# One ring slot's reload moved behind the team's last down product, in a mixture-of-experts stage on one Trainium2 core

## The reference

```python
router_logits = x @ gate_w                                   # 256 x 64
routing_weights, selected = jax.lax.top_k(router_logits, 8)
routing_weights = jax.nn.softmax(routing_weights, axis=-1)
...
gate = jax.lax.ragged_dot(hidden_sorted, gate_proj_w, group_sizes)    # 64 experts, 512 x 192
up = jax.lax.ragged_dot(hidden_sorted, up_proj_w, group_sizes)        # 64 experts, 512 x 192
down = jax.lax.ragged_dot(jax.nn.silu(gate) * up, down_proj_w, group_sizes)   # 192 x 512
...
out = jnp.sum(out * routing_weights[..., None], axis=1)
return x + out
```

## Time and profile before

| | |
|---|---|
| median of 3 runs | 325.79 us |
| the profiled execution, device time | 328.78 us |
| its span, first to last instruction | 327.1 us |
| TensorE busy in the span | 301.1 us, 92% |
| VectorE busy | 166.9 us, 51% |
| ScalarE busy | 100.7 us, 31% |
| mean granted TensorE clock | 0.974 of full |
| weights and other data moved by SP's queue | 83.51 MB |

### The profile page before, as it was taken

One profiled execution on the slowest core, in us unless ns is written; L12 is line 12 of the kernel. 1 busy time (PEld: TensorE's weight loads), 2 busy tenths in 40 slices (PEclk: granted clock), 3 DMA queues, 4 the chain that ended last, 5 costly groups with the idle time before them and its releaser, 6 DMA issues.

```text
span 327.1 us, 8833 instructions
## 1 busy us (share of the span) xinstructions
PE 301.1 (92%) x2667; PEld 170.6 (52%) x2667; DVE 166.9 (51%) x567; ACT 100.7 (31%) x198; POOL 77.2 (24%) x183
## 2 busy tenths in 40 slices
PE   0499999989899999799999999999999999999994
PEld 0364444435577545436555655565556555655561
DVE  7752366495468585424534453445344534453443
ACT  1020400212748134313333333333333323332332
POOL 5000000340000033442233224222422233223322
PEclk9999999999669999959999999999999999999999
DMA  2699995930000010691999999999999999999921
GB/s 70 242 429 397 386 394 193 373 108 2 2 0 4 0 42 25 217 376 43 358 386 390 392 382 392 353 394 393 385 393 390 373 371 387 385 394 384 392 85 66
DMA packets 42363, 87.85 MB, mean 269 GB/s; under 512 B 6023, under 2 KB 14351, under 8 KB 42208
## 3 DMA queue, kind: packets, MB, share of 16 engines
q1 hardware_dynamic: 39600, 83.51, 68.9%
q0 software_dynamic: 2320, 3.95, 3.4%
q10 hardware_dynamic: 416, 0.04, 0.1%
HBM read 90.09 MB, written 1.05 MB: 279 GB/s over the span
## 4 chain that ended last, share of the span: by engine, by line
PE 83%; DVE 9%; ACT 3%; issue 2%; POOL 1%; POOLq 1%; DVEq 0%; ACTq 0%
PE psum L1343 22%; PE psum L1399 17%; PE psum L1273 10%; PE psum L1091 5%; PE psum L1130 4%; PE psum L1103 4%; PE psum L1386 4%; PE psum L1380 2%; PE psum L1191 2%; PE psum L1221 2%; PE psum L1082 2%; ACT store L971 2%; PE psum L1175 1%; PE psum L1245 1%; PE psum L1366 1%
## 5 line engine op out<-in xcount | busy, mean ns | idle before, releaser
L1343 PE MATMUL psum<-store 128*32 128x384 f32 x896 | 80.1, 496 | 0.6 <-issue 0.6
L1399 PE MATMUL psum<-store 128*32 128x256 f32 (+1 forms) x672 | 54.9, 459 | 0.4 <-DVE store L888 0.4
L1343 PEld LDWEIGHTS psum<-store 128*32 128x32 f32 x896 | 35.1, 112 | 33.3 <-issue 30.2
L902 DVE SCALAR_TENSOR_TENSOR y_parts<-psum,w_slot,y_parts 128x512 fp32r<-128x512 f32 x28 | 21.0, 751 | 54.4 <-ACT y_parts L1045 54.4
L1045 ACT ACTIVATE y_parts<-psum,w_slot 128x512 fp32r<-128x512 f32 x28 | 19.2, 687 | 57.0 <-PE psum L1399 52.9
L1273 PE MATMUL psum<-y_parts,place_T 128*128 128x512 f32 x112 | 33.8, 422 | 0.9 <-ACT y_parts L1045 0.8
L1399 PEld LDWEIGHTS psum<-store 128*32 128x32 f32 x672 | 23.0, 110 | 20.1 <-issue 8.5
L571 POOL DMA_INDIRECT store<-x_normed_rows,row_no x29 | 29.7, 1024 | 15.0 <-issue 15.0
L1273 PEld LDWEIGHTS psum<-y_parts,place_T 128*128 128x128 f32 x112 | 18.8, 188 | 21.2 <-DVE y_parts L902 14.2
L570 POOL TENSOR_TENSOR ready<-zero 128x1 f32<-128x1 f32 x29 | 5.6, 193 | 98.2 <-DVE row_no L869 98.2
L1013 ACT ACTIVATE store<-psum 128x512 f32<-128x512 f32 x29 | 17.3, 597 | 34.8 <-PE psum L1386 31.7
(11 more groups left out here) (247 smaller groups left out, 398.8 us busy)
## 6 DMA issues: line engine op xcount, KB each, us to landing
store<-n_L_ffn_gate_proj_w_dram SPq DMA_DIRECT2D x64, 384.0 KB
store<-in_L_ffn_up_proj_w_dram SPq DMA_DIRECT2D x64, 384.0 KB
store<-n_L_ffn_down_proj_w_dram SPq DMA_DIRECT2D x64, 256.0 KB
store<-n_L_ffn_down_proj_w_dram SPq DMA_DIRECT2D x64, 128.0 KB
store<-in_L_attn_w_qkv_dram SPq DMA_DIRECT2D x1, 3072.0 KB, 15.0
store<-in_ctx_dram SPq DMA_DIRECT2D x2, 1024.0 KB, 6.5
store<-in_L_attn_w_out_dram SPq DMA_DIRECT2D x1, 1024.0 KB, 17.3
x_sb<-in_x_dram SPq DMA_DIRECT2D x1, 512.0 KB, 4.4
```

Source lines behind the costliest of these rows:

```text
L902: dve.scalar_tensor_tensor(y_parts[:, 1], bank[6], w_slot[:, :], y_parts[:, 0], ALU.mult, ALU.subtract).then_inc(s_yl, 1)
L1343: last = pe.matmul(bank[0][quarter, 0:2 * INTER], xs[:, c, quarter], w[:, :, c, :], start=(c == 0), stop=(c == DC - 1))
L1399: last = pe.matmul(bank[6][quarter, cols], hidT[:, k, quarter], ring[r][:, e, at:at + cols.stop - cols.start], start=(k == 0), stop=(k == 2))
```

## The change

`reload` waits once, for `s_y`, and then issues the 16 transfers of the slot lane by lane: gate, up and the two down parts of expert 0, then those of expert 1, and so on. Sizes, addresses and semaphores of the transfers stay as they were, and so do the loads of teams 0 to 3 and all other engines.

```diff
-            def load_gate_up(team, r):
+            def load_gate_up(team, r, first=0):
                 loaded = []
-                for j, e in enumerate(team):
+                for j, e in enumerate(team, first):
                     loaded.append(e)
                     lane = ring[r][:, j]
...
-            def load_down(team, r):
-                for j, e in enumerate(team):
+            def load_down(team, r, first=0):
+                for j, e in enumerate(team, first):
                     lane = ring[r][:, j]
...
                 team = list(team_of(word_of(q)))
-                sp.wait_ge(s_gu, sp.snap(done))
-                load_gate_up(team, r)
                 sp.wait_ge(s_y, sp.snap(done))
-                load_down(team, r)
+                for j, e in enumerate(team):
+                    load_gate_up([e], r, j)
+                    load_down([e], r, j)
```

## The result

The changed kernel took **331.89 us**, the median of 4 runs (328.76 to 333.33), beside 325.88 us before: ratio 1.0195, 95% interval 1.0137 to 1.0253. It is slower by 6.0 us, in the range and to the side that was given, 2.2 us over the point. The profiled execution took 333.33 us, span 331.6. The title names one ring slot; the edit is to all 12 calls of `reload`, and it changes the order of each one's 16 transfers as well as the wait.

A forecast was written before the change was run, and what follows sets the result against it. TensorE was taken to bound the last stage. The stream 3.97 us later and gate and up 3.3 us further back, against 3.5 us of slack, gave a 3.8 us stall: 325.8 + 3.9 = 329.7 us, range 325.4 to 333.6.

The forecast's parts named there:

- What bounds the kernel: Last stage: TensorE bounds it, a round every 6.547 us; the transfers only have to keep ahead.
- The wait moves the stream by 3.97 us and nothing absorbs it: First reload starts at 157.6, not 153.65; the transfers end 3.97 us later; later waits cause no second loss.
- one slowest DMA engine that never runs dry: Weight stream: the slowest of 16 engines sets the pace, from 155 to 315 us with nothing missing, 13.35 us a team.
- The order adds 3.3 us for gate and up: End of each reload: 1.1 us of transfers behind the last gate and up instead of 4.4, so they land 3.3 us later.
- the slack of 3.5 us: Last round: gate and up there at about 310.8, wanted at 314.33, leaving 3.5 us.
- The clock taken at 0: TensorE behind the last round's stall: half clock could cost 0 to 2.9 us; 0 was taken.
- rival B: Last round: stall plus half clock behind it, 329.7 + 2.9 = 332.6 us; chance 0.30.
- A: Last round: no stall outside the profile, time unchanged at 325.8 us; chance 0.27 together with the edit doing nothing.
- C: Reloads: mixed row sizes run a few per cent slower on the slowest engine, 334 to 337 us; chance 0.06.
- D: Expert rounds: less load on SBUF shortens each of 25 rounds by 0.04 us, 324.8 us or less; chance 0.04.

The follow-up runs named there:

- experiment 5: Kernel before with the wait for s_y ahead of gate and up in the first reload alone: 326.38 us, ratio 0.9988, runs in two heaps.
- experiment 7: Changed kernel with each of GpSimd's indirect fetches of token rows replaced by a memset: 327.37 us, one run.
- Experiment 2: Kernel before with one wait for s_y ahead of every reload, transfers in the old order: 327.15 us, ratio 1.0058.
- experiment 3: Kernel before with the new wait and lane-by-lane order in the last team's reload alone: 326.07 us, ratio 1.0029.
- experiment 9: Changed kernel with 5 useless matmuls in TensorE's 1.08 us self attention gap: 327.66 us.
- 11: Kernel before with the later wait alone, old order, plus 5 useless matmuls in the self attention gap: 323.04 us.
- experiment 8: Kernel before with 5 useless matmuls in TensorE's 1.08 us self attention gap: 321.63 us, ratio 0.9898.
- 12: Kernel before with 5 useless matmuls in the self attention gap and 5 in the 1.27 us gap of the first round of experts: 321.38 us, ratio 0.986.
- 6: Changed kernel with the last team's 16 transfers back in the old order behind the same wait: 326.83 us, ratio 1.0035.
- 1: Changed kernel run again without edit: 331.76 us, median of 6 runs.
- 4: Changed kernel with 18 useless matmuls ahead of the last team's wait for gate and up: 329.69 us.
- 10: Changed kernel with 5 useless matmuls in the self attention gap and 18 in the gap ahead of the last round: 325.99 us.

## Why the prediction came out as it did

**What bounds the kernel**: right. TensorE kept its beat of 6.55 us in every round but the last.

**The wait moves the stream by 3.97 us and nothing absorbs it**: right. The data end 4.1 us later against the beat, the first reload is issued 154.81 - 150.65 = 4.16 us behind the third round's gate and up, as forecast (157.6 - 153.45), and experiment 5 shows that the first reload alone brings a gap of the same kind. The cause I gave for it, one slowest DMA engine that never runs dry, is shown in part: experiment 5's tail has one engine of 16 at work alone. That this engine was busy without a pause since round 3 was only argued, as the profile has no view by engine, and experiment 7 leaves open what slows it. (The round that starts at 255.41 is the 19th, not the 18th; nothing hangs on it.)

**The order adds 3.3 us for gate and up**: right in kind, near in size. Let s be the slack, w the delay by the wait and o that by the order. Experiment 2 gives w - s = 1.1, experiment 3 o - s = 0.35, and experiments 9 to 11 give w + o - s = 4.4. The third less the other two is s = 4.4 - 1.1 - 0.35 = 2.95, and so w = 4.05 and o = 3.3. These three figures aren't of one kind (an idle time, a late start, a difference of medians), so they are good to some 0.3 us. The traces allow a direct check, since they keep the moment of every rise of a semaphore. The last rise of `s_wg[3]`, which lets the last team start, in us from the third round's start, one figure for each profile:

| kernel | last gate and up landed |
|---|---|
| before (some of its records are missing); experiments 8 and 12 | 160.75; 160.37, 160.34 |
| order alone, last reload (experiment 3) | 163.73 |
| wait alone (experiments 2 and 11) | 164.77, 164.78 |
| changed, last reload in the old order (6) | 164.53 |
| first reload's wait alone (5) | 166.00 |
| changed, without the fetches (7) | 164.96 |
| changed (result, 1, 4, 9 and 10) | 167.99, 167.42, 167.74, 167.60, 167.28 |

On its beat the last round starts at 314.33 - 150.66 = 163.67, and a start follows the landing by 0.21 us (315.85 to 316.06), so gate and up are wanted at 163.46. The slack is 2.7 to 3.1 us, the wait takes 4.0 to 4.4 of it and the order 3.0 to 3.4. **The terms w and o were as predicted, the slack of 3.5 us was mis-sized.** I had put the landing at 310.8 - 150.66 = 160.1, which is 0.2 to 0.6 us too early, and had the start at once behind it, 0.2 us more. With that the last round starts 4.0 to 4.6 us late in the five profiles of the changed kernel, and not 3.8.

**The clock taken at 0**: the step that failed. It read "I take 0: the matmuls ahead of the gap are the dense ones, as at 68.7". The gap at 68.7 was 1.56 us, this one 4.4; the other row, a stretch with 2.2 us of idleness ahead of half clock, was no farther off. And the profile of before held a third that the prediction leaves out: the one gap of 1.08 us at 83 us with 10.2 us at half clock behind it (experiment 8), which spoke against 0. The runs show 1.7 us in the median and 2.8 in the profile, inside the bounds of 0 to 2.9; single runs of experiment 9 exceed them, by how much through the clock isn't shown. Here the Trainium skill's rule (TensorE: Matmul & The Clock Gate, HAM oscillation) was right and I set it aside: a wait of 3.8 to 4.4 us on a transfer did take the clock to 1.2 GHz in the three profiles in which nothing filled it (granted clock 0.50 behind it). The result lies between the forecast (329.7) and rival B (332.6), nearer to B.

**The rivals.** A (no stall off the profile) fell: all the single runs, not the profiled ones alone, show the cost. What looks like A, the single run of 325.89, is the gap's cost on top of the lower level. B happened in most executions. C fell with experiment 6. D: the beat went from 6.547 to 6.544 us, 0.07 us in 24 rounds, so no gain. On the lag that A hangs on, the Trainium skill (DMA: Bandwidth & Descriptors, Latency and other measured facts) says that two of the DMA engines are usually slower than the rest and, as a best guess, ties that to transfers issued by GpSimd. Experiment 7, in which the traffic ends some 3 us earlier without these, fits it, without showing it.

## What to carry to other kernels

Where a stream of loads feeds an engine and is close to it in pace, find the last load and its first user: a delay in a stream that never pauses arrives there whole (4.0 us at round 3 of 28 here), and the order inside the last load decides what is left. Put first what is used first, gate and up ahead of down, as long as the user waits for all lanes anyway. Price a new gap on TensorE with the clock behind it, and look for the gaps that are already there: five matmuls of no use in one gap of 1.08 us gave more (4.2 us) than the gap was long.

## What the runs showed of the hardware

The kernel before, left alone, has two levels, about 321.5 and 325.8 us, and 9 of its 69 runs beside the experiments lie at the lower one and one between, at 323.55. The levels come from one stretch of 10 us at half clock behind a gap of 1.08 us, which in other executions has full clock behind it; filling the gap left only the lower one. What decides between the two in an execution isn't shown. A gap of some 4 us doesn't have the same cost every time either: the changed kernel at the one level ranges from 325.87 to 330.35 us, and with the gap filled from 325.58 to 326.72. At the end of a stream the engines don't finish together: in experiment 5 a single one of 16 is left for 2 us, at 24 GB/s.
